# A gated cross-attention and mixture-of-experts layer: where sixteen late tiles of the shared expert are done, and by which counts the last loads wait

## The chip, the cores and the metric

The kernel runs on one core of a Trainium2 chip. The core has five engines that run their own instruction streams and wait for one another by semaphores: TensorE (PE, matmuls), VectorE (DVE), ScalarE (ACT), GpSimd (POOL) and SyncE (SP, which here only reads registers and issues DMAs). The metric is the device time of one execution in microseconds (us), lower is better. Before the change the median of three runs is 305.51 us (304.73 to 306.84).

## The reference

`x` holds 2 x 1024 tokens of 256 numbers. The layer adds gated cross-attention to it, and then a gated feed-forward part: a shared expert for all tokens, and two of eight experts for each token.

```python
x = x + tanh(g_xattn) * attention(layernorm(x), ctx)        # 16 heads, 64 keys
h = layernorm(x)                                            # 2048 tokens
scores = sigmoid(h @ W_gate_router)
sel = top_k(scores + expert_bias, 2); w = scores[sel] / sum(scores[sel])
shared = silu(h @ Wg_s) * (h @ Wu_s) @ Wd_s                 # hidden width 192
routed_k = silu(h @ Wg[sel_k]) * (h @ Wu[sel_k]) @ Wd[sel_k]
x = x + tanh(g_ffn) * (shared + w_0 * routed_0 + w_1 * routed_1)
```

## The kernel before

All arithmetic is in float32; where more speed is wanted, an operand is split into a high and a low part of the faster format and three products are made of them (`split_product`). Tokens are worked on in T = 16 tiles of 128.

**Token loop.** Each of the steps t = 1 to 15 (`token_loop`, one `step(t, q)` for each engine) interleaves several tiles: TensorE transposes tile t+2, makes the shared expert's hidden layer and the router's logits of tile t-2 (`shared_up`), transposes the probabilities of tile t, makes the scores of tile t+2 and the attention output of tile t. In the last two steps there is no tile t+2 any more. Behind the loop tiles 14 and 15 are finished: second layer norm, `shared_up`, the choice of experts, the counting of places (`rank`, `count`), and the tables that say which expert each expert tile has and where its rows lie (`tables` on VectorE). GpSimd writes each token's normalised row to `rows_dram`, once for each of its two experts, at its place in the expert's area.

**Late tiles.** The hidden layer of the shared expert stays in SBUF (`late_hid`) for all tiles. What is left of a tile is late work: TensorE transposes the hidden layer (`late_transpose`, two transposes), ScalarE copies that to `lhT` (`late_hidden`), TensorE multiplies by `Wds` (`late_down`, two matmuls), ScalarE copies the result to `late_out` (`late_copy`), GpSimd adds it to `x_sb` (`late_add`). Tiles 0 to NB - 1 = 11 go this way between the token loop and the expert loop. `late_out` is the same memory as `plane[1]`, below.

**Expert loop.** `expert_loop` runs over SLOT_TILES = 39 places for expert tiles of 128 rows (steps j = -4 to 40; the number that hold rows depends on the data). For each tile SP loads 128 gathered rows, at an address that it reads from `tile_src` four tiles ahead; TensorE transposes them, multiplies by the expert's weights, ScalarE and VectorE make the hidden layer, TensorE multiplies by `Wd` (step j + 2), ScalarE copies the result to one of four buffers, and GpSimd scatters it by an indirect DMA to `routed_dram`, which has a row for each token and choice. Semaphores `scattered[0]` to `scattered[3]` count the scatters of each buffer.

**Planes and tail.** Then SP loads `routed_dram` back in chunks of PLANE = 4 token tiles, first the first choice (plane 0, in order of expert number), then the second (plane 1). Before each load it waits until enough tiles are scattered: `turns[c]` holds four counts, which VectorE worked out in steps 1 to 3 from the places that chunk c's tokens occupy (`tiles_up_to`, `last_turns`, `count_turns`), and which SP reads from SBUF into registers, four reads for a row (`turn_values`). The counts of plane 0 leave out expert 7, which nobody has as first choice. Plane 1 has one row of counts for all four chunks, the largest of all:

```python
sp.wait_ge(scattered[r], turns[min(n, T // PLANE)][r])   # n = 0..3 plane 0, 4..7 plane 1
```

For tiles 0 to 11 VectorE adds both planes to `x_sb` with the tokens' weights (`add_low` for plane 0, L1328 for plane 1), and the pairs of tiles are stored. Tiles 12 to 15 go another way: their late work is done in steps 39 and 40 and behind the loop, their product stays open in PSUM, and TensorE adds three more products to it (`tail_sum`, L1442): the identity times the `x_sb` rows, and two diagonal matrices of the weights (`diag`, made by ScalarE in steps 32 to 39) times the planes. ScalarE copies the sums (L926) and the last stores follow. SP issues two of the eight stores, ScalarE six.

**What sets the order.** Each engine does its instructions in the order in which this code issues them; SP's register reads, waits and DMA issues stand in one such order too. There is no scheduler.

## Time and profile before

| | before |
|---|---|
| median of the runs | 305.51 us |
| lowest and highest run | 304.73 and 306.84 us |
| span of the profiled execution (first to last instruction) | 304.1 us |
| TensorE busy | 274.8 us (90%) |
| VectorE busy | 239.4 us (79%) |
| GpSimd busy | 172.6 us (57%) |
| ScalarE busy | 160.7 us (53%) |
| DMA traffic | 49.74 MB |

The profile shows one execution, with times in us from the start of its span; that execution is not one of the timed runs. A share of busy time is a mean over stages: up to about 160 us the token loop, to 197 us the end of routing and the late tiles, to 292 us the expert loop, and the tail to 304. What a change in one of them is worth is read from the waits in that stage.

### The profile page before, as it was taken

The numbers are of one execution on the slowest core, as the hardware profiler recorded it, in microseconds if no ns is written. First come the engines' busy times: TensorE is split into PE (matmuls) and PEld (weight loads), VectorE is DVE, ScalarE is ACT, GpSimd is POOL, SyncE is SP. The second block draws the span as 40 slices with busy tenths as digits, with TensorE's granted clock in tenths as the row PEclk, the third lists the DMA queues.
The fourth block names the chain that finished last, engine by engine and source line by source line (L and its number), as shares of the span: only waits on it lengthen the run. The fifth ranks groups of instructions, "written<-read, shape, count | busy, mean of one in ns | idle before, by whom it ended". The sixth has DMA issues, their size and how long they took to land.

```text
span 304.1 us, 6562 instructions
## 1 busy us (share of the span) xinstructions
PE 274.8 (90%) x1746; PEld 246.3 (81%) x1747; DVE 239.4 (79%) x691; ACT 160.7 (53%) x414; POOL 172.6 (57%) x234
## 2 busy tenths in 40 slices
PE   2899989999999999999996668988799999999994
PEld 1788767998897898999886657877699899999883
DVE  0489989899899789899989565479877777777684
ACT  1452475656666566564453433654455555566731
POOL 8012225777758886897855876648544344444430
PEclk9999999999999999999999999999999999999999
DMA  6999994123359999923121122323343434446796
GB/s 185 361 288 314 306 293 140 41 77 100 103 167 302 312 286 318 270 69 106 35 70 56 59 81 90 105 56 86 90 118 111 123 96 122 121 114 167 249 325 232
DMA packets 45006, 49.74 MB, mean 164 GB/s; under 512 B 3928, under 2 KB 41650, under 8 KB 44978
## 3 DMA queue, kind: packets, MB, share of 16 engines
q1 hardware_dynamic: 39938, 39.37, 45.5%
q0 software_dynamic: 3408, 8.46, 8.1%
q10 hardware_dynamic: 1632, 1.57, 1.5%
q8 instruction: 13, 0.21, 0.3%
q14 instruction: 15, 0.12, 0.1%
HBM read 21.67 MB, written 28.64 MB: 165 GB/s over the span
## 4 chain that ended last, share of the span: by engine, by line
PE 60%; DVE 24%; issue 8%; ACT 4%; DMA 2%; SPq 1%; ACTq 0%; DVEq 0%
PE bank L1401 7%; PE bank L1403 6%; PE bank L1402 5%; PE scores_ps L1401 5%; PE scores_ps L1403 4%; PE scores_ps L1402 4%; DVE row_max L1146 3%; DVE probs L1152 3%; DVE row_sum L1136 3%; PE bank L1347 3%; DVE pT_lo L1129 3%; PE scores_ps L1438 2%; PE bank L1598 2%; DMA Wq_sb<-in_L_xattn_Wq_dram 2%; PE bank L1438 2%
## 5 line engine op out<-in xcount | busy, mean ns | idle before, releaser
L699 POOL DMA_INDIRECT routed_dram<-probs,sct_idx x39 | 38.1, 977 | 49.3 <-ACT probs L911 46.8
L649 POOL TENSOR_TENSOR probs<-probs,row_inv 128x1024 f32<-128x1024 f32 x16 | 30.5, 1909 | 26.4 <-DVE row_inv L1140 26.3
L613 POOL DMA_INDIRECT rows_dram<-xn,slot_i x32 | 32.0, 1000 | 14.0 <-issue 10.5
L1401 PE MATMUL bank<-AB_hi,pT_hi 128*128 128x256 f32 x128 | 37.0, 289 | 2.4 <-DVE pT_lo L1129 2.4
L1403 PE MATMUL bank<-AB_hi,pT_lo 128*128 128x256 f32 x128 | 35.8, 279 | 0.0
L1402 PE MATMUL bank<-AB_lo,pT_hi 128*128 128x256 f32 x128 | 35.7, 279 | 0.0
L768 ACT ACTIVATE probs<-probs 128x1024 f32<-128x1024 f32 x16 | 17.0, 1061 | 29.5 <-DVE probs L1152 25.4
L1401 PE MATMUL scores_ps<-AB_hi,xnT_hi 128*128 128x512 f32 x64 | 27.0, 421 | 2.5 <-DVE xnT_lo L1122 2.3
L1401 PEld LDWEIGHTS bank<-AB_hi,pT_hi 128*128 128x128 f32 x128 | 24.1, 188 | 3.0 <-issue 2.9
L1403 PE MATMUL scores_ps<-AB_hi,xnT_lo 128*128 128x512 f32 x64 | 25.3, 395 | 0.0
L1402 PE MATMUL scores_ps<-AB_lo,xnT_hi 128*128 128x512 f32 x64 | 25.3, 395 | 0.0
L1129 DVE TENSOR_TENSOR pT_lo<-bank,pT_hi 128x512 fp32r<-128x512 f32 x32 | 20.5, 682 | 5.6 <-ACT pT_hi L776 5.3
L1402 PEld LDWEIGHTS bank<-AB_lo,pT_hi 128*128 128x128 f32 x128 | 24.1, 188 | 0.0
L1403 PEld LDWEIGHTS bank<-AB_hi,pT_lo 128*128 128x128 f32 x128 | 24.1, 188 | 0.0
L1299 DVE TENSOR_TENSOR xnT_lo<-bank,xnT_hi 128x256 fp32r<-128x256 f32 x39 | 16.6, 425 | 6.9 <-ACT xnT_hi L888 5.8
L776 ACT ACTIVATE pT_hi<-bank 128x512 fp32r<-128x512 f32 x32 | 17.3, 595 | 6.6 <-PE bank L1500 6.4
L1152 DVE TENSOR_TENSOR probs<-scores_ps,row_max 128x1024 f32<-128x1024 f32 x16 | 19.5, 1216 | 0.1
L1136 DVE TENSOR_REDUCE row_sum<-probs 128x16 f32<-128x1024 f32 x16 | 19.4, 1210 | 0.1
L1146 DVE TENSOR_REDUCE row_max<-scores_ps 128x16 f32<-128x1024 f32 x16 | 19.2, 1200 | 0.0
L1401 PEld LDWEIGHTS scores_ps<-AB_hi,xnT_hi 128*128 128x128 f32 x64 | 12.0, 188 | 6.7 <-DVE xnT_lo L1122 4.5
L1401 PE MATMUL bank<-W_hi,xnT_hi 128*128 x40 | 15.4, 386 | 1.9 <-DVE xnT_lo L1299 1.9
L1401 PE MATMUL scores_ps<-W_hi,xnT_hi 128*128 x38 | 14.6, 384 | 2.6 <-DVE xnT_lo L1299 2.6
(248 smaller groups left out, 876.6 us busy)
## 6 DMA issues: line engine op xcount, KB each, us to landing
rows_dram<-pad_rows SPq DMA_DIRECT2D x10, 1040.0 KB, 16.5
rows_dram<-pad_rows SPq DMA_DIRECT2D x8, 780.0 KB, 12.2
AB_free<-routed_dram SPq DMA_DIRECT2D x8, 512.0 KB, 6.4
probs<-rows_dram SPq DMA_DIRECT2D x30, 130.0 KB
raw_buf<-in_L_ffn_Wg_dram SPq DMA_DIRECT2D x8, 192.0 KB, 2.5
raw_buf<-in_L_ffn_Wu_dram SPq DMA_DIRECT2D x8, 192.0 KB, 2.6
out_dram<-x_sb ACTq DMA_DIRECT2D x6, 256.0 KB, 2.9
pT_hi<-rows_dram SPq DMA_DIRECT2D x9, 130.0 KB
```

Of the source, the lines that this page charges most:

```text
L613: nc.gpsimd.indirect_dma_start(rows_dram[:, :], bass.IndirectOffsetOnAxis(ap=slot_i[:, t, k:k + 1], axis=0), xn2[:, t % KEEP, :], None).th ...
L649: nc.gpsimd.tensor_tensor(pr, pr, row_inv[:, :].unsqueeze(2).to_broadcast([P, H, KV]), ALU.mult).then_inc(norm_done, 1)
L699: nc.gpsimd.indirect_dma_start(routed_dram[:, :], bass.IndirectOffsetOnAxis(ap=sct_idx[(k - 2) % (2 * RING)][:, 0:1], axis=0), y_sb[ks][:, ...
L768: nc.scalar.activation(prob[m % 2][:, :], prob[m % 2][:, :], ACT.Exp).then_inc(exp_done, 1)
L776: nc.scalar.activation(pT_hi[:, 4 * h:4 * h + 4, :], pT_ps[h][:, :].rearrange("p (c s) -> p c s", c=4), ACT.Copy).then_inc(pT_hi_done, 1)
L1129: nc.vector.tensor_tensor(pT_lo[:, 4 * h:4 * h + 4, :], pT_ps[h][:, :].rearrange("p (c s) -> p c s", c=4), pT_hi[:, 4 * h:4 * h + 4, :].bi ...
L1136: nc.vector.tensor_reduce(row_sum[:, :], prob[m % 2][:, :].rearrange("p (h k) -> p h k", k=KV), AX_X, ALU.add).then_inc(sum_done, 1)
L1146: nc.vector.tensor_reduce(row_max[:, :], by_head, AX_X, ALU.max).then_inc(max_done, 1)
L1152: nc.vector.tensor_tensor(prob[u % 2][:, :].rearrange("p (h k) -> p h k", k=KV), by_head, row_max[:, :].unsqueeze(2).to_broadcast([P, H, KV]),
L1401: nc.tensor.matmul(out_ap, a_hi, b_hi, start=first, stop=False)
L1402: nc.tensor.matmul(out_ap, a_hi, b_lo, start=False, stop=False)
L1403: return nc.tensor.matmul(out_ap, a_lo, b_hi, start=False, stop=last)
```

## The change

All late work is done ahead of the expert loop; none is left behind it. In parts:

- Late tiles 0 to 3 (EARLY) are done inside and right behind the last two token steps, with other PSUM banks, `lhT` for two tiles at once, and copies of two tiles at once into parts of `late_hid` that are no longer needed (`late_row`). Tiles 4 to 15 take the places of tiles 0 to 11 between the loops. GpSimd adds all sixteen in steps 0 to 7.
- NB is 10 instead of 12: TensorE sums six tiles (10 to 15), VectorE adds the planes of ten. A sum now starts with the `x_sb` rows (`tail_rows`) and takes the planes' products (`tail_plane`); rows and plane 0 of tiles 10 to 14 stand in steps 39 and 40. GpSimd makes the twelve diagonals, two per step behind the scatters of steps 32 to 37.
- Plane 1 has a row of counts for each chunk. SP reads the four rows in the tail, each in front of its chunk's load.
- SP reads the first four tile addresses before it waits for the scattered rows. TensorE counts the last batch before the wide sum (`last_ps`) instead of after it.

```diff
-NB = 12
+NB = 10
+EARLY = 4
...
-        CHUNK_ROWS = T // PLANE + 1
+        CHUNK_ROWS = TOPK * T // PLANE
...
             sp.wait_ge(tile_src_done, 1)
-            for r in range(KEEP):
-                sp.wait_ge(rows_put[r], 16 * TOPK * T // KEEP)
             sp.wait_ge(pads_put, 16)
...
                     sp.load(src_regs, tile_src[0:1, bass.ds(n, RING)])
                     sources[:] = [sp.snap(r, min_val=0, max_val=PAD_TILE * P) for r in src_regs]
+                if isinstance(n, int) and n == 0:
+                    for r in range(KEEP):
+                        sp.wait_ge(rows_put[r], 16 * TOPK * T // KEEP)
...
                     n = k * (T // PLANE) + c
-                    if n == T // PLANE - 1:
-                        turns.append(turn_values(chunk_turns[0:1, T // PLANE, :]))
+                    if k:
+                        turns.append(turn_values(chunk_turns[0:1, n, :]))
                     for r in range(RING):
-                        sp.wait_ge(scattered[r], turns[min(n, T // PLANE)][r])
+                        sp.wait_ge(scattered[r], turns[n][r])
                     if k:
-                        sp.wait_ge(late_added, NB)
+                        sp.wait_ge(late_added, T)
                     load_plane(sp, k, c * PLANE, PLANE, (plane1_loaded if k else plane0_loaded)[c])
...
+            def weighted_ident(n):
+
+                nc.gpsimd.tensor_scalar(diag[n], ident[:, :], weight[:, NB + n // 2, n % 2:n % 2 + 1], None, ALU.mult).then_inc(diag_done, 1)
...
-                    for z in range(max(0, 2 * j), min(2 * j + 2, NB)):
+                    for z in range(max(0, 2 * j), min(2 * j + 2, T)):
                         late_add(z)
+                n = 2 * (j - (SLOT_TILES - T + NB - 1)) if isinstance(j, int) else -1
+                if 0 <= n < 2 * (T - NB):
...
+                    weighted_ident(n)
+                    weighted_ident(n + 1)
...
+            def early_hidden(z):
+                act.wait_ge(lhT_ps_done, z + 2)
+                after(act, late_done, z)
+                nc.scalar.activation(lhT_both[:, :, :, :].rearrange("p q k s -> p (q k) s"),
+                                     scores_ps[0:FH, 512:1024].rearrange("p (k s) -> p k s", k=4), ACT.Copy).then_inc(lhT_done, 2)
+
+            def early_copy(z):
+                act.wait_ge(late_done, z + 2)
+                act.wait_ge(lhT_ps_done, ((z + 2) * D + F - 1) // F)
+                nc.scalar.activation(used_hid[:, z * D:(z + 2) * D], scores_ps[:, 0:512], ACT.Copy).then_inc(late_read, 2)
...
+                    if t == T - 2:
+                        early_hidden(0)
                     if t == T - 1:
+                        early_hidden(2)
+                        early_copy(0)
                         round_down(3)
...
-                chain(nc.vector.tensor_reduce(chunk_slots[:, T // PLANE:], chunk_turn.rearrange("o c e -> o (c e)"), AX_X, ALU.max))
+                chain(nc.vector.tensor_reduce(chunk_slots[:, T // PLANE:], chunk_turn, AX_X, ALU.max))
...
-                    late_transpose(NB)
-                    late_transpose(NB + 1)
+                    tail_rows(NB)
+                    tail_rows(NB + 1)
                 if isinstance(j, int) and j == SLOT_TILES + 1:
-                    late_down(NB)
-                    late_transpose(NB + 2)
-                    late_down(NB + 1)
+                    for z in range(NB + 2, T - 1):
+                        tail_rows(z)
+                    for z in range(NB, T - 1):
+                        tail_plane(0, z)
...
             expert_loop(pe, expert_step)
-            late_transpose(NB + 3)
-            late_down(NB + 2)
-            late_down(NB + 3)
+            tail_rows(T - 1)
+            tail_plane(0, T - 1)
             for z in range(NB, T):
-                tail_sum(z, ident[:, :], x_sb[:, z, :])
...
+                tail_plane(1, z)
```

How the order moves is shown at three places. The first is SP's queue behind its last gather for the expert loop. `AB_free<-routed_dram` is a plane load, `chunk_turns` a read of one count (four for a row, each followed by two register instructions). Before:

```order
L408 DMA AB_free<-routed_dram 128x4x256 x3
L487 TENSOR_LOAD chunk_turns
L487 ISA x2
...
L408 DMA AB_free<-routed_dram 128x4x256 x5
L402 DMA out_dram<-x_sb 128x2x256 x2
```

And with the change, where the left-out lines are the other three reads of a row:

```order
L414 DMA AB_free<-routed_dram 128x4x256 x4
L493 TENSOR_LOAD chunk_turns
L493 ISA x2
...
L414 DMA AB_free<-routed_dram 128x4x256
L493 TENSOR_LOAD chunk_turns
L493 ISA x2
...
L414 DMA AB_free<-routed_dram 128x4x256
L408 DMA out_dram<-x_sb 128x2x256
```

The one row of counts stood between the third and the fourth load; now a row stands in front of each of the last four.

The second place is TensorE's queue from step 40 on. L1411 ends an expert tile's last product; `lhT` and `late_hid` with `ident` are late work, `x_sb` with `ident` the rows of a sum, and `late_hid` with `AB_free` a diagonal with a plane. Before, from the late work in front of the last expert tile:

```order
L1438 MATMUL bank<-Wds,lhT 128x256 x2
L1431 MATMUL bank<-ident,late_hid 96x128 x2
L1438 MATMUL scores_ps<-Wds,lhT 128x256 x2
...
L1411 MATMUL bank<-AB_hi,pT_lo 128x256
L1431 MATMUL bank<-ident,late_hid 96x128 x2
L1438 MATMUL scores_ps<-Wds,lhT 128x256 x2
L1438 MATMUL bank<-Wds,lhT 128x256 x2
L1442 MATMUL bank<-x_sb,ident 128x256
L1442 MATMUL scores_ps<-x_sb,ident 128x256 x2
```

With the change, from the same place to the end:

```order
L1467 MATMUL scores_ps<-x_sb,ident 128x256 x2
L1467 MATMUL bank<-x_sb,ident 128x256
L1473 MATMUL bank<-AB_free,late_hid 128x256 x2
L1473 MATMUL scores_ps<-AB_free,late_hid 128x256 x2
L1473 MATMUL bank<-AB_free,late_hid 128x256
...
L1434 MATMUL bank<-AB_hi,pT_lo 128x256
L1467 MATMUL bank<-x_sb,ident 128x256
L1473 MATMUL bank<-AB_free,late_hid 128x256 x3
L1473 MATMUL scores_ps<-AB_free,late_hid 128x256 x2
L1473 MATMUL bank<-AB_free,late_hid 128x256 x2
```

Late work has left the tail; rows and plane 0 of the sums moved ahead of the last expert tile, and behind it stand one tile's rows and plane 0 and then the six products with plane 1.

The third place is TensorE's queue in token step 15. L1500 transposes the probabilities, the `Wsh` rows are `shared_up`, the `mask` and `carry` rows `rank`, `bank<-ident,xn` the transposes of a normalised tile. Before:

```order
L1500 MATMUL bank<-ident,probs 128x128 x8
L1401 MATMUL bank<-AB_hi,pT_hi 128x256
...
L1464 MATMUL bank<-carry,ones_r 128x16
L1401 MATMUL bank<-Wsh_hi,xn2T_hi 128x392
...
L1431 MATMUL bank<-ident,late_hid 96x128 x4
L1471 MATMUL bank<-ident,xn 128x128 x2
```

With the change:

```order
L1531 MATMUL bank<-ident,probs 128x128 x8
L1461 MATMUL scores_ps<-Wds,lhT_both 128x256 x2
L1424 MATMUL bank<-AB_hi,pT_hi 128x256
...
L1495 MATMUL bank<-carry,ones_r 128x16
L1461 MATMUL scores_ps<-Wds,lhT_both 128x256 x2
L1454 MATMUL bank<-ident,late_hid 96x128 x2
L1424 MATMUL bank<-Wsh_hi,xn2T_hi 128x392
...
L1461 MATMUL scores_ps<-Wds,lhT_both 128x256 x2
L1454 MATMUL bank<-ident,late_hid 96x128 x2
L1502 MATMUL bank<-ident,xn 128x128 x2
```

A late product now stands ahead of the attention of tile 15, one with two transposes behind the ranking, and another such pair where two pairs of transposes stood. In step 14 there are, in the same manner, four transposes ahead of the attention, and a product with four transposes behind it.

## Rows read from the trace of the kernel before

**Rows 1.** Chain that ended last, tail: start, us, what it went through.

```profile
292.45 0.22 PE bank L1431 x2
292.66 0.87 PE scores_ps L1438 x4
...
298.28 0.86 PE scores_ps L1442 x4
299.14 0.45 PE bank L1442 x2
299.59 0.66 ACT x_sb L926 x2
```

**Rows 2.** A stretch: us, busy (count) of PE, PEld, DVE, ACT, POOL; granted clock; DMA.

```profile
220.00:280.00 60.00, 59.51 (x410) 56.72 (x410) 44.15 (x163) 35.46 (x113) 26.28 (x27) 1.00 0.41 117
```

**Rows 3.** SP's plane loads: start, us, queue, line (the first of x2 starts there).

```profile
278.00 0.38 SPq L408 DMA_DIRECT2D AB_free<-routed_dram  x1
...
286.11 0.36 SPq L408 DMA_DIRECT2D AB_free<-routed_dram  x1
287.51 0.98 SPq L408 DMA_DIRECT2D AB_free<-routed_dram  x2
289.29 0.38 SPq L408 DMA_DIRECT2D AB_free<-routed_dram  x1
```

**Rows 4.** Reads of turn counts between 279 and 282 us: ns, first and last start.

```profile
L487 SPq TENSOR_LOAD <-chunk_turns x4: 267/278/340, 279.5 to 281.3; - x4
L487 SPq SEQ_ASSERT  x4: 18/18/23, 280.1 to 281.8; - x4
```

**Rows 5.** Issue to landing: the last plane load; then the last four stores.

```profile
DMA to landing us min/median/max: 7.2/7.2/7.2
DMA to landing us min/median/max: 2.2/2.9/3.4
```

**Rows 6.** Timeline around the tail: start, us, instruction, idle before and its releaser.

```profile
282.94 0.97 POOL L699 DMA_INDIRECT routed_dram<-probs,sct_idx  x1 [1.15 <-ACT probs L911]
...
291.50 0.47 PE L1407 MATMUL bank<-AB_hi,pT_lo 128*128 x1
292.12 1.67 DVE L1328 SCALAR_TENSOR_TENSOR x_sb<-AB_free,weight,x_sb 128x256 f32<-128x256 f32 x4 [0.91 <-DMA AB_free<-routed_dram]
...
300.28 0.39 ACTq L402 DMA_DIRECT2D out_dram<-x_sb  x1
```

**Rows 7.** An early stretch by engine, and eight transposes early and late.

```profile
3.00:5.00 2.00, 0.00 (x0) 0.00 (x0) 0.00 (x0) 0.00 (x0) 1.88 (x2) 1.00 0.96 284
6.80 1.97 PE L1357 MATMUL bank<-ident,Wq_sb 128*128 128x128 f32 x8 [0.67 <-DVE bias_cols L938]
170.61 1.04 PE L1500 MATMUL bank<-ident,probs 128*128 128x128 f32 x8
```

**Rows 8.** TensorE in the last token steps: first matmuls after an idle time.

```profile
169.42 0.45 PE L1401 MATMUL bank<-Wsh_hi,xn2T_hi 128*128 128x392 f32 x1 [1.29 <-DVE xn2T_lo L1103]
172.71 0.35 PE L1401 MATMUL bank<-AB_hi,pT_hi 128*128 128x256 f32 x1 [1.07 <-DVE pT_lo L1129]
178.11 0.45 PE L1401 MATMUL bank<-Wsh_hi,xn2T_hi 128*128 128x392 f32 x1 [1.68 <-DVE xn2T_lo L1103]
```

**Rows 9.** The expert loop's start: SP's last wait, first gather, TensorE's first transposes.

```profile
L492 SPq EVENT_SEMAPHORE  x1: 28/28/28, 193.1 to 193.1; - x1
194.50 0.37 SPq L504 DMA_DIRECT2D probs<-rows_dram  x1
197.46 0.60 PE L1598 MATMUL bank<-ident,probs 128*128 128x128 f32 x4
```

**Rows 10.** Additions on GpSimd beside VectorE's index operation, and that operation alone.

```profile
209.73 1.44 POOL L689 TENSOR_TENSOR x_sb<-AB_free,x_sb 128x256 f32<-128x256 f32 x2
210.39 0.80 DVE L1309 SCALAR_TENSOR_TENSOR sct_idx<-probs,tile_e 128x1 int32<-128x1 f32 x1
219.63 0.21 DVE L1309 SCALAR_TENSOR_TENSOR sct_idx<-probs,tile_e 128x1 int32<-128x1 f32 x1
```

More of the change, by code:

```diff
@@ L87, in flamingo_layer @@
         Wds = sb("Wds", [FH, 2, D])
-        lhT = [sb(f"lhT{q}", [FH, 2, P]) for q in range(2)]
+        lhT_both = sb("lhT_both", [FH, 2, 2, P])
+        lhT = [lhT_both[:, q, :, :] for q in range(2)]
         ident = sb("ident", [P, P])
@@ L1320, in _ @@
             expert_loop(dve, expert_step)
-            for c in range(NB // PLANE):
+            for c in range((NB + PLANE - 1) // PLANE):
                 if c:
@@ L1325, in _ @@
                 dve.wait_ge(plane1_loaded[c], 16)
[L1326 removed]
+                for t in range(c * PLANE, min((c + 1) * PLANE, NB)):
                     dve.wait_ge(plane0_added, t + 1)
```

116 lines of the change are left out of this document (61 added, 55 removed).

## The prediction, made before the changed kernel ran

> **What bounds the kernel now.** I read the chain that ended last first, from its end. After the last tile of the expert loop it runs through TensorE alone: late tiles (L1431 two transposes, L1438 the product with `Wds`), then the twelve sums of L1442, then ScalarE's copies [rows 1]. So the end hangs on TensorE. The table by stage says the same of the loop: 59.5 of 60 us busy between 220 and 280 us [rows 2]. From the loop's end the profile gives prices: a late tile costs TensorE 0.87 us for its product and 0.22 for its transposes, a sum 0.43 to 0.45 [rows 1].
>
> Next I read SP's queue, because it issues the eight plane loads (0.5 MB each). Plane 0's chunk 0 goes at 278.0 and its chunk 3 at 286.1; plane 1's chunks 0, 1, 2, 3 go from 287.5 to 289.3, three steps in 1.78 us, so 0.59 from each to the next [rows 3]. The one row of four turn counts that SP reads here (L487) lies between plane 0's chunk 2 and chunk 3, from 279.5 to 281.8: 2.3 us for four reads [rows 4]. It costs nothing there, since chunk 3 goes only at 286.1, when the expert tiles that it needs have been scattered.
>
> Then landings. Plane 1's chunk 3 lands 7.2 us after its issue at 289.3, so at 296.5 [rows 3, 5]. TensorE's last four sums are its last 4 x 0.43 = 1.7 us before 299.6, so from 297.9 [rows 1]: that load has 1.4 us to spare. From the last sum (299.6) to the end of the span (304.1) are 4.5 us: copy, store issue at 300.3, a landing of up to 3.4 us [rows 5, 6].
>
> **The change part by part. The turn counts.** Plane 1's chunks now wait each for its own count, read by SP in front of each of plane 1's four loads. I look first at what finer counts can bring. Worked out from the reference's own inputs: the eight experts hold 1943, 28, 2048, 0, 0, 0, 0 and 77 token pairs, so 34 tiles, and expert 7's single tile is the last. Each chunk of 512 tokens has some of the 77 (17, 19, 28 and 13). A count for plane 1 is the largest over all eight experts, hence 34 for every chunk, the number that all four waited for before. Nothing is released earlier. The trace agrees: the scatter of that tile (the 34th) starts at 282.9 [rows 6], plane 1's chunk 0 goes at 287.5, and the three others follow without a wait [rows 3].
>
> What it costs: the reads move behind the issue of plane 0's chunk 3, where nothing hides them. Each of the four loads now comes 2.3 + 0.59 = 2.9 us after the one before: 289.0, 291.9, 294.8, 297.7. Chunk 0's tiles have long been scattered by 289.0. The last load goes at 297.7 instead of 289.3, +8.4 us. (Other rows of reads are not cheaper by more than a tenth or two; I use 2.3.)
>
> How long it then takes to land is not shown for a load with no other close to it. Bounds: 2.2 us, the quickest 256 KB store [rows 5], and 7.2. Between them: plane 1's chunk 0, with others issued 1.4 us before and 0.6 after it, released VectorE at 292.1, 4.6 us after its issue [rows 3, 6]. I take 3.8, since twice a store's bytes must cost more than 2.2 and fewer neighbours less than 4.6. It lands at 301.5, and token tiles 12 to 15 need it.
>
> **The sums.** TensorE has six tiles to sum instead of four, but the x rows and plane 0 come inside steps 39 and 40: three terms for six tiles are 18 x 0.43 = 7.8 us, against 4 late tiles and 12 sums before (4.4 + 5.2 = 9.6). By 295 all is done that does not need plane 1: before, the last expert tile's product began at 291.5 [rows 6]; eight sums (3.4 us) now stand in front of it in place of 2.0 us of late work, and two more sums follow it. VectorE has 20 additions of 0.42 (1.67 for four [rows 6]) instead of 24, 1.7 us less. Neither is worth anything at the end, since both now wait for plane 1. Left after 301.5 are four sums.
>
> **TensorE's rate in those four.** From 295 to 301.5 it has only the two sums that need plane 1's chunk 2. What does it run at after that? The granted clock reads 1.00 (2.4 GHz) everywhere, even between 3 and 5 us, where TensorE had no instruction. But the spacing of equal rows says otherwise: eight 128x128 transposes take 1.97 us at 6.8 us, shortly after the engine's first work, and 1.04 at 170.6 [rows 7]. That is the 1.2 GHz level after idleness. I take the doubled spacing for the four sums: 4 x 0.86 = 3.4 us, ending at 305.0; with the undoubled one 1.7 us, ending at 303.2. The Trainium skill ("TensorE: Matmul & The Clock Gate", Part 1) has the rule for it: the throttled state is the default, and only activity lifts it. By that rule the doubled case holds and the sum below is the higher one; by the granted clock column alone it is the lower. After the last sum I take 3.7 us instead of 4.5, as the final stores have fewer neighbours (2.5 instead of 3.4, between 2.2 and 3.4 [rows 5]). The span's end from this part: 308.7, so +4.6 (undoubled: 306.9, +2.8).
>
> **Four late tiles in the last two token steps.** They go into TensorE's idle times there, which end at 169.4 (1.29 us), 172.7 (1.07) and 178.1 (1.68) [rows 8]. Into the first go a product and four transposes, 0.87 + 0.44 = 1.3; into the second a product, 0.9; into the third a product and two transposes, 1.1. The fourth product and its pair of transposes replace the two pairs that stood ahead of token tile 15's transposes (1.1 for 0.44). The first gap is full, the others nearly: +0.2, between 0 and 0.6. ScalarE's wider copies stand where it waits for TensorE. If this cover is gone, what is late next is the normalised token tile 15, and through it all routing.
>
> **Ahead of the expert loop.** Twelve late tiles are there before and after, in one pattern, and TensorE goes from them to the first expert tile without idling at 197.5 [rows 9]. SP reads the tile addresses before its wait for the scattered rows, not behind it: wait over at 193.1, first gather at 194.5 [rows 9]. Up to 0.9 of these 1.4 us go. But the gather isn't what TensorE waits for, so 0 (bound -0.9). The count before the wide sum: at most 0.1, likewise hidden: 0.
>
> **In the loop.** GpSimd adds all sixteen tiles by step 7, four more than before, 0.72 each. VectorE's index operation takes 0.80 beside such an addition at 210.4 [rows 10] against some 0.2 elsewhere; two such steps, mostly out of phase: +0.1 (0 to 0.6). The diagonals move from ScalarE to GpSimd, two per step behind its scatter. A 128x128 product by GpSimd is not shown; between nothing and the 0.72 of an addition of twice the width. Two at most 1.44 plus 0.97 for the scatter [rows 6] pass the tile's 2.1 us only at that bound: 0 (to +0.5). ScalarE isn't waited for in those steps: 0.
>
> **Sum.** 4.6 + 0.2 + 0.1 = +4.9 on the span of 304.1, so 309.0. The runs' median of 305.51 lies 1.4 above the span; I carry this along: 310.4 us.
>
> **The rivals.** *Full rate*: the same wait for SP, but the sums at 0.43. For it: the granted clock, never under 1.00, and two sums that interrupt the idleness. Against it: [rows 7]. 310.4 - 1.8 = 308.6.
> *Not slower*: SP's reads cost little, because they are quicker there or the sequencer gets ahead. With loads at their old spacing the last one lands by 296.5 and the last four sums end at 298.2 instead of 299.6: -1.4; with +0.3 in front 304.4. It decides at the read: the end stays at 304.1 if the last load lands at 298.4, so goes at 294.6, a quarter of 8.5 us each, 1.5 us for four reads instead of 2.3. For it: only that a single TENSOR_LOAD shows 0.27 us; against it: starts 0.6 apart [rows 4].
> *An earlier loop*: the first gather does decide, and 0.9 come back: 309.5. Against it: no idle time at 197.5 [rows 9].
> *Late token steps*: the inserted tiles and GpSimd's additions cost their upper bounds of 0.6 and 0.6: +0.9 over my sum, 311.3. For it: gaps that are filled to the brim.
>
> **How the numbers follow.** Chances: my sum 0.38, full rate 0.32, late token steps 0.12, earlier loop 0.10, not slower 0.08. The range: full rate with a quick landing (-0.7) and a short store (-0.5) gives 307.4 at the low end; my sum with a landing of 4.6 (+0.8) and the front's bounds (+0.9) gives 312.1 at the high end. Some 2 in 10 are left out, the case "not slower" among them. A measurement of this kernel can tell about 1% (3.1 us, so 308.6) from no change. Slower by over 1%: my sum, the late steps, 0.07 of the earlier loop and half of full rate make 0.73, of which I keep 0.70. Within 1%: the other half of full rate, the rest of the earlier loop and "not slower" make 0.27, of which I keep 0.25. Faster by over 1%: no mechanism gives it; 0.05 for what I have not seen.
>
> **What would show it.** Four reads between each of plane 1's load issues, 2.9 us apart, the last near 298; VectorE and TensorE idle for them; four last sums 0.86 apart (or 0.43); token steps and the loop's start within 0.6 us of before. It is wrong if plane 1's last load goes before 295, or if the end of the span still follows TensorE's sums without a gap.

## The result, and the profile after

The changed kernel takes 312.58 us (median of 4 runs, 311.52 to 312.95), the kernel before 305.12 beside it (304.58 to 306.84). The ratio is 1.023, with a 95% interval of 1.019 to 1.027: the change makes the kernel slower. Predicted were 310.4 us with a range that ended at 312.1. Side and mechanism were right; the size was 2.2 us too small. Here and below the medians are of all runs, while a ratio and its interval leave out the runs that lay over 1.5% above the fastest run of their kernel.

| | before | after |
|---|---|---|
| median of the runs | 305.12 us | 312.58 us |
| profiled execution: span | 304.1 us | 310.1 us |
| first exponential of the token loop starts | 33.57 us | 34.20 us |
| plane 1's last load is issued | 289.29 us [rows 3] | 298.31 us |
| last store is issued | 300.28 us [rows 6] | 307.48 us |
| granted clock, mean of the span | 1.000 | 0.981 |

From the page of after: the span, TensorE's granted clock in 40 slices, and two of the queues (packets, MB, share).

```profile
span 310.1 us, 6641 instructions
...
PEclk9999999999999999999999999999999999999975
...
q8 instruction: 13, 0.21, 0.3%
```

The row of the clock ends in 7 and 5; in the page of before, which the prediction had read, it stands at 9 to the end. The queue q8 comes back below.

SP's timeline in after (start, us, queue, line): plane 0's last load and plane 1's four. They answer to [rows 3].

```profile
285.86 0.36 SPq L414 DMA_DIRECT2D AB_free<-routed_dram  x1
...
288.67 0.36 SPq L414 DMA_DIRECT2D AB_free<-routed_dram  x1
...
291.43 0.36 SPq L414 DMA_DIRECT2D AB_free<-routed_dram  x1
...
294.17 0.36 SPq L414 DMA_DIRECT2D AB_free<-routed_dram  x1
...
298.31 0.36 SPq L414 DMA_DIRECT2D AB_free<-routed_dram  x1
```

Three steps of 2.7 to 2.8 us, as predicted (2.9), and a last one of 4.1. What fills them are SP's reads of the counts: in after, those of the third row and of the fourth (ns: min, median, max; first and last start).

```profile
L493 SPq TENSOR_LOAD <-chunk_turns x4: 261/266/285, 291.8 to 293.5; - x4
...
L493 SPq TENSOR_LOAD <-chunk_turns x4: 265/634/934, 294.6 to 297.0; - x4
```

The third row's reads answer to [rows 4]: 0.27 us for one read, 0.57 from one to the next. The fourth row has a read of 0.93.

The last load's landing (DMA view of after: KB, median us to landing), against 7.2 in [rows 5]:

```profile
AB_free<-routed_dram SPq DMA_DIRECT2D x1, 512.0 KB, 4.8
```

TensorE's sums with plane 1 in after (timeline: start, us, tile, count of matmul instructions, two for a sum; idle time before them and its releaser), then stretches of 10 us (busy time of PE, PEld, DVE, ACT, POOL; granted clock, DMA share, GB/s):

```profile
299.40 2.05 PE L1473 MATMUL bank<-AB_free,late_hid 128*128 128x256 f32 x4 [5.90 <-DMA AB_free<-routed_dram]
303.28 2.04 PE L1473 MATMUL scores_ps<-AB_free,late_hid 128*128 128x256 f32 x4 [1.82 <-DMA AB_free<-routed_dram]
305.12 1.91 PE L1473 MATMUL bank<-AB_free,late_hid 128*128 128x256 f32 x4
```

```profile
280.00:290.00 10.00, 9.82 (x63) 8.95 (x62) 7.47 (x26) 4.84 (x15) 9.13 (x13) 1.00 0.58 194
290.00:300.00 10.00, 4.10 (x21) 3.36 (x20) 6.50 (x17) 0.38 (x1) 3.06 (x4) 0.92 0.80 263
300.00:310.00 10.00, 5.20 (x12) 3.14 (x10) 0.17 (x1) 2.30 (x6) 0.00 (x0) 0.50 0.46 153
```

Where TensorE was busy to the last sum before [rows 1], it now stands idle for 5.9 us and again for 1.8, both times for a plane load. The sums then stand 0.92 us apart instead of 0.43, at a granted clock of 0.50, which is the 1.2 GHz level.

One fact is needed for comparing executions: the first exponential of the token loop starts between 31.8 and 34.7 us, whichever kernel runs, and this alone spreads the spans by over 2 us. So times inside the kernel are counted from that exponential from here on:

| us behind the first exponential | before | after | after, another run (e11) |
|---|---|---|---|
| first expert tile's copy | 171.2 | 170.1 | 170.2 |
| plane 0's last load issued | 252.5 | 251.7 | 252.5 |
| plane 1's last load issued | 255.7 | 264.1 | 264.2 |
| last sum ends | 266.0 | 272.8 | 272.9 |
| end of the span | 270.5 | 275.9 | 276.0 |

The loop comes 1.1 us sooner, the last load 8.4 later, the end 5.4 later. Under e6 it turns out that the 1.1 us belong to the profiled execution of before, which came late to its loop, and not to the change; counted from the first expert tile's copy, the end comes 6.4 us later (99.3 in before, 105.8 in after and e11). The other 3.0 of the last load's 8.4 come back behind it: before, it landed among other loads, after 7.2 us, and the stores were crowded too.

### The profile page after: what moved, and what is told of

Same layout as the page of the kernel before. It is cut to its first block, busy times and chain, and to the rows that moved or that the text cites. A ratio compares the mean times of both kernels' runs of the same rounds, so it can differ in the third digit from the quotient of the medians.

```text
span 310.1 us, 6641 instructions
## 1 busy us (share of the span) xinstructions
PE 281.3 (91%) x1758; PEld 250.3 (81%) x1759; DVE 237.8 (77%) x687; ACT 159.7 (52%) x408; POOL 183.0 (59%) x250
## 4 chain that ended last, share of the span: by engine, by line
PE 54%; DVE 23%; issue 8%; DMA 6%; ACT 4%; POOL 3%; SPq 1%; POOLq 0%; DVEq 0%; ACTq 0%
PE bank L1424 5%; PE scores_ps L1424 5%; PE bank L1426 5%; PE bank L1425 5%; PE scores_ps L1426 4%; PE scores_ps L1425 4%; DVE row_max L1169 3%; DVE probs L1175 3%; PE bank L1370 3%; DVE row_sum L1159 3%; DVE pT_lo L1152 3%; DMA Wk_sb<-in_L_xattn_Wk_dram 3%; PE bank L1641 2%; PE bank L1392 2%; POOL rows_dram L620 2%
## 5 line engine op out<-in xcount | busy, mean ns | idle before, releaser
L794 ACT ACTIVATE pT_hi<-bank 128x512 fp32r<-128x512 f32 x32 | 17.3, 595 | 6.6 <-PE bank L1531 6.4
L1531 PE MATMUL bank<-ident,probs 128*128 128x128 f32 x128 | 16.6, 273 | 0.0
```

The lines of the kernel that those rows point to most:

```text
L794: nc.scalar.activation(pT_hi[:, 4 * h:4 * h + 4, :], pT_ps[h][:, :].rearrange("p (c s) -> p c s", c=4), ACT.Copy).then_inc(pT_hi_done, 1)
```

## The experiments

Each ran beside the kernel before, whose medians were 304.99 to 305.58 us. "Last copy" is ScalarE's copy of the last expert product; "tail" runs from its start to the end of the span: 11.6 us in before (292.5 to 304.1) and 17.4 in after (292.7 to 310.1).

### The reads alone: e1, e2, e10, e7

**e1**: after with the old single row of counts for plane 1, read ahead of plane 0's last load.

```diff
...
-                    if k:
-                        turns.append(turn_values(chunk_turns[0:1, n, :]))
+                    if n == T // PLANE - 1:
+                        turns.append(turn_values(chunk_turns[0:1, T // PLANE, :]))
                     for r in range(RING):
-                        sp.wait_ge(scattered[r], turns[n][r])
+                        sp.wait_ge(scattered[r], turns[min(n, T // PLANE)][r])
...
```

> The changed kernel with one edit undone: plane 1 has one row of counts again, read by SP ahead of plane 0's last load. All else stays changed. Theory A (SP's four rows of reads behind plane 0's last load delay plane 1's last load, which then idles TensorE): the last plane load goes near 289 instead of 298.3, TensorE's last sums are 0.43 us apart again, the span ends near 302 to 303, 7 to 8 us under the changed kernel's 310.1 and 1 to 2 under before's 304.1. Rival B (the six sums on TensorE, or the diagonals on GpSimd, make the tail long whatever SP does): the span stays above 307.

307.08 us; ratio 1.003 (0.999 to 1.007). Plane 1's loads go 0.54 apart again, the last 2.2 us behind plane 0's last. TensorE's timeline in e1:

```profile
295.64 1.10 PE L1473 MATMUL bank<-AB_free,late_hid 128*128 128x256 f32 x4 [0.72 <-DMA AB_free<-routed_dram]
297.08 1.10 PE L1473 MATMUL scores_ps<-AB_free,late_hid 128*128 128x256 f32 x4 [0.34 <-DMA AB_free<-routed_dram]
```

With the reads out of the way the idle time is 0.7 instead of 5.9 us, the sums stand 0.43 to 0.5 apart, and nearly all of the loss is gone. The other parts of the change together cost at most 0.7%.

**e2**: the reverse, before with nothing but a row of counts for each of plane 1's loads, read in the tail.

```diff
...
-                    if n == T // PLANE - 1:
-                        turns.append(turn_values(chunk_turns[0:1, T // PLANE, :]))
+                    if k:
+                        turns.append(turn_values(chunk_turns[0:1, n, :]))
...
```

> The kernel before with that one edit alone: a row of counts for each chunk of plane 1, read in the tail. Theory A: plane 1's last load goes near 297.5 instead of 289.3, lands some 4.9 us later, and TensorE, which has been idle by then, ends its four sums near 306; span 308 to 310, +4 to +6 on 304.1. Rival B: under +1.5, since before has no diagonals on GpSimd and four sums only.

310.42 us; ratio 1.012 (1.000 to 1.025). The tail is 16.1 us, 4.5 more than in before; loads at 284.09, 286.90, 289.67, 292.42 and 295.82. TensorE in e2:

```profile
300.53 1.22 PE L1442 MATMUL bank<-AB_free,late_hid 128*128 128x256 f32 x2 [4.13 <-DMA AB_free<-routed_dram]
301.54 1.91 PE L1442 MATMUL scores_ps<-AB_free,late_hid 128*128 128x256 f32 x4
```

So this one edit brings the idle time and the halved rate by itself, without any of the moved tiles.

**e10**: after, with each of plane 1's rows read one load earlier, so that three stand behind plane 0's last load.

```diff
-                    if k:
-                        turns.append(turn_values(chunk_turns[0:1, n, :]))
+                    if T // PLANE - 1 <= n < TOPK * T // PLANE - 1:
+                        turns.append(turn_values(chunk_turns[0:1, n + 1, :]))
```

> After, with the four rows of plane 1 each read one load earlier: the first ahead of plane 0's last load, so that three rows are left behind it. Theory A (what stands behind that load costs 2.3 each): the last plane-1 load goes 2.8 us sooner against plane 0's last one, 9.0 to 9.7 instead of 12.4, and the end 2.5 to 3.0 us sooner. On the row that was slow in after, e2 and e3 (the fourth, 3.4 to 4.1 us from load to load in place of 2.8): if it is slow because of what runs beside it at that time (the stores of the first half and the last scatters, some 8 to 11 us behind plane 0's last load), the fourth row, read now at 5.5 to 8.5, takes 2.8 like the others, and the last load goes at 8.9 or sooner; if it is its place in SP's program, it stays at 3.4 or more, and the last load goes at 9.2 or later.

309.51 us, against 311.45 for after beside it (e11). The last load goes 8.8 us behind plane 0's last one, 12.4 in after and 11.7 in e11: one row less is worth 3.6 and 2.9 us there, more than 2.8, since the fourth row is quick now. It ends at 294.1; all of its four reads take 0.26 to 0.28 us. So its place in SP's program isn't what made it slow. In after, e2 and e11 the slow read starts where GpSimd's last scatter and the first stores are on the way. Which of these slows it was not separated.

**e7**: e1 with its single row behind plane 0's last load.

```diff
-                    if n == T // PLANE - 1:
+                    if n == T // PLANE:
                         turns.append(turn_values(chunk_turns[0:1, T // PLANE, :]))
```

> After, with a single row of turn counts for plane 1 (as in before), but read behind the issue of plane 0's last load instead of ahead of it: one row on the path, where after has four and the earlier run with the row ahead has none. Theory A (each row that is read behind plane 0's last load moves plane 1's loads by its 2.3 us): the first plane-1 load comes 2.8 us after plane 0's last, the three others 0.55 apart, so the last 4.5 after it (2.2 with the row ahead, 12.4 in after); TensorE idles over 2 us ahead of its plane-1 sums, and the end comes 1.5 to 2.4 us later than with the row ahead. Rival B (the loss in after comes from waiting four times, not from the reads): the last load goes within 0.5 us of the run with the row ahead.

Loads: 2.83 us behind plane 0's last one, then 0.54, 0.54 and 0.56, the last 4.47 behind: as the reads' price has it. TensorE in e7:

```profile
296.29 1.10 PE L1473 MATMUL bank<-AB_free,late_hid 128*128 128x256 f32 x4 [3.32 <-DMA AB_free<-routed_dram]
297.67 1.80 PE L1473 MATMUL scores_ps<-AB_free,late_hid 128*128 128x256 f32 x4 [0.27 <-DMA AB_free<-routed_dram]
```

The last store is issued 9.5 us behind the last copy, in e1 6.2. The end did not follow: 305.83 us, not slower than e1 (307.08). Two things hide the row there. Eight of e1's ten runs, but only three of e7's, took 2.4 us or more beyond their spans instead of 1.7 to 1.9, which the section on e11 to e13 explains. And in e1 the profiled span ended 5.2 us behind its last store (2.7 in e7), after a last scatter by GpSimd that took 4.02 us instead of 1.0. What the end waits for there is not a load, a sum or a store, but GpSimd's DRAIN, the instruction with which each engine closes (ns; first and last start). It lasts until 305.2; SP's, which comes last in e7 and in before, was done at 303.0:

```profile
L67 POOLq DRAIN  x1: 10122/10122/10122, 295.1 to 295.1; - x1
L67 SPq DRAIN  x1: 13/13/13, 303.0 to 303.0; - x1
```

So the price of a row is shown at the loads and the sums, not in the median.

### The clock: e3, e5

**e3** and **e5** keep TensorE busy in after while it waits: products into a bank that nobody reads, ahead of the plane-1 sums (20 in e3, 12 in e5, and 5 more ahead of tile 12).

```diff
             tail_plane(0, T - 1)
+            pe.wait_ge(ycopy_done, SLOT_TILES)
+            for n in range(12):
+                nc.tensor.matmul(bank[0][:, 0:D], ident[:, :], x_sb[:, T - 1, :], start=True, stop=True)
             for z in range(NB, T):
+                if z == T - PLANE:
+                    for n in range(5):
+                        nc.tensor.matmul(bank[0][:, 0:D], ident[:, :], x_sb[:, T - 1, :], start=True, stop=True)
                 tail_plane(1, z)
```

> The changed kernel with 25 extra products of 256 columns on TensorE into a spare bank while it waits for plane 1's last two loads; their result is not used. Theory A's second half (TensorE is at the lower clock when the last load lands): the last four sums are 0.43 us apart instead of 0.92, the granted clock stays 1.00 to their end, span 1.5 to 2 us under 310.1. Rival C (the sums are slow for another reason, as waiting on memory): spacing stays 0.9, span within 0.5 us of 310.1.

311.8 us, mean clock 1.000. The last four sums take 0.43 each, but the fillers ended at 302.9 and 305.9, later than the loads landed: the rate was gained and lost again.

> After, with 12 filler products (0.43 us each, into a bank that nobody reads) between the last plane-0 sum and the plane-1 sums of tiles 10 and 11, and 5 more ahead of those of tiles 12 to 15; the earlier run with 20 and 5 kept the clock but its fillers ended later than the landings. Theory A (the four sums run at half the clock because TensorE stood idle while SP read the rows): fillers end before the landings at about 299.4 and 303.2, the last four sums take 0.43 each in place of 0.92, and the tail from the last expert copy to the end falls from 17.4 to 15.4 to 16.0 us; the median falls by 1.4 to 2.0 us against after. Rival B (the landing of the last load alone decides, and the sums at half rate are hidden behind stores): tail unchanged, 17.4 within 0.4.

308.48 us; ratio 1.010 (1.005 to 1.016). TensorE in e5:

```profile
295.06 5.34 PE L1681 MATMUL bank<-x_sb,ident 128*128 128x256 f32 x24
300.81 1.10 PE L1473 MATMUL bank<-AB_free,late_hid 128*128 128x256 f32 x4 [0.41 <-DMA AB_free<-routed_dram]
301.75 2.32 PE L1685 MATMUL bank<-x_sb,ident 128*128 128x256 f32 x10
303.91 1.03 PE L1473 MATMUL scores_ps<-AB_free,late_hid 128*128 128x256 f32 x4
```

The tail falls from 17.4 to 14.7 us. From the issue of the last load to the end of the last sum it takes 6.8 instead of 8.7: 1.9 us, the doubled rate of four sums. The rest of the 2.7 comes from loads that went 0.6 to 1.0 sooner against the last copy in this execution. So useless work makes the kernel faster (the median is also 2.6 us below that of e13, which ran on another chip, with longer code too but without fillers in the tail), and the halved rate is worth 1.9 us of its end. The rival by which the landing alone decides is out.

### The parts that were costed at nothing: e6, e9, e4, e8

**e6**: before, with only SP's read of the source addresses moved ahead of its wait for the rows.

```diff
             sp.wait_ge(tile_src_done, 1)
-            for r in range(KEEP):
-                sp.wait_ge(rows_put[r], 16 * TOPK * T // KEEP)
 ...
+                if isinstance(n, int) and n == 0:
+                    for r in range(KEEP):
+                        sp.wait_ge(rows_put[r], 16 * TOPK * T // KEEP)
```

> Before, with one edit of the change alone: SP reads the source addresses of its first gathers ahead of its wait for the rows, in place of behind it. Theory A (this read stood between the last row and the first gather): the first expert transposes come 0.9 us sooner against the first exponential of the token loop (33.6 in place of 34.5 us behind the first tile's, by the trace: 197.1 less 162.9 against 197.5 less 163.9), and the end as much sooner if nothing else holds it: -0.9 us. Rival B (the 0.9 comes from the shared expert's tiles having been moved, or from PE): the loop starts where it did, 0 within 0.2.

ScalarE's timeline: the first exponential and the first expert copy in before, then in e6.

```profile
33.57 1.05 ACT L768 ACTIVATE probs<-probs 128x1024 f32<-128x1024 f32 x1
...
204.80 0.38 ACT L911 ACTIVATE probs<-bank 128x256 f32<-128x256 f32 x1
```

```profile
33.82 1.05 ACT L769 ACTIVATE probs<-probs 128x1024 f32<-128x1024 f32 x1
...
204.06 0.38 ACT L912 ACTIVATE probs<-bank 128x256 f32<-128x256 f32 x1
```

171.23 us before and 170.24 in e6: the loop starts 1.0 us sooner, and the profiled span counted from the exponential is 269.5 instead of 270.5. The number expected came, but by luck: the gather is not its cause. e2, in which SP has the old order, shows it. Its first exponential, its first gathers and its first expert transposes:

```profile
31.85 1.05 ACT L768 ACTIVATE probs<-probs 128x1024 f32<-128x1024 f32 x1
191.50 1.43 SPq L504 DMA_DIRECT2D probs<-rows_dram  x3
195.73 0.60 PE L1598 MATMUL bank<-ident,probs 128*128 128x128 f32 x4
```

Counted from the exponential, e2's first gather goes 1.3 us sooner than before's (159.65; 194.50 in [rows 9] is 160.93), and its transposes start at the same 163.88 (before 163.89). In e6 the gather goes at 158.32 and the transposes start at 163.01; TensorE comes to them from the late work without idle time in all three. In e6 TensorE was 0.7 us ahead of before already when the last ranking began, at 151.93 instead of 152.64, which is 4.8 us ahead of SP's read of the addresses. Some 9 us earlier VectorE had waited for TensorE in before, and in e6 it had not:

```profile
176.64 0.42 DVE L1109 TENSOR_TENSOR x_sb<-bank,x_sb 128x256 f32<-128x256 f32 x1 [0.76 <-PE bank L1403]
```

```profile
176.00 0.43 DVE L1110 TENSOR_TENSOR x_sb<-bank,x_sb 128x256 f32<-128x256 f32 x1
```

e2 has no such wait, but loses as much in a later stretch ahead of its loop, at a granted clock of 0.51:

```profile
180.60:183.90 3.30, 3.30 (x11) 2.94 (x11) 1.18 (x9) 0.78 (x3) 2.53 (x3) 0.51 0.36 122
```

So the loop hangs on TensorE's late work and not on the first gather, as the prediction had it [rows 9], and the 1.0 us was lost in single executions ahead of anything that the edit touches. Why both executions with the old order lost it, at different places, and none of the fourteen with the new one, stays open. The twelve runs agree that there is no gain: 305.64 us, ratio 1.002 (0.999 to 1.006).

**e9**: after with the diagonals on ScalarE, as in before.

```diff
...
-                    weighted_ident(n)
-                    weighted_ident(n + 1)
...
+                    for m in (n, n + 1):
+                        nc.scalar.activation(diag[m], ident[:, :], ACT.Copy, scale=weight[:, NB + m // 2, m % 2:m % 2 + 1]).then_inc(diag_done, 1)
```

> After, with one edit undone: the twelve weighted diagonals are made by ScalarE, as in before, and not by GpSimd. Theory A (two diagonals of 0.6 each and a scatter of 1.03 make GpSimd's turn 2.44 us, longer than the tiles' 2.13, so that the scatters of tiles 28 to 33 slip by about 1.0 us): the scatters of the last tiles stand 2.1 to 2.2 apart, the first of the SP's four plane-0 chunks to be waited for last is issued about 1.0 us sooner against the last expert copy, and the median falls by 0.8 to 1.2. Rival B (the scatters had 1.3 us in hand, and SP's loads wait for the very last scatter, which is bounded by the last expert product): 0 to -0.3.

On GpSimd two diagonals and a scatter make 2.44 us a tile, more than the tile's 2.13. With ScalarE the scatter of tile 33 does start 1.1 us sooner against the copy of tile 36 (tiles counted from 0; 5.30 ahead of it, 4.24 in after). But plane 0's last load goes at 6.80 us ahead of the last copy, in after 6.82, and the tail is 17.3. By the semaphores in the trace this load waits for the scatter of the tile ahead of that one, 32 (expert 7's tile 33 is left out of plane 0's counts): its last count comes 0.02 us ahead of the load in both. With ScalarE that scatter starts 0.4 us sooner against the copy of tile 36 (7.12 ahead of it, 6.68 in after), but it lands 6.1 us behind its start instead of 5.7, both times beside plane 0's first three loads. Late scatters cost nothing here: the prediction's zero holds, though GpSimd came nearer to the bound than its row let expect. The median of 310.11 (spans of 306.8 to 309.9) is 1.3 below e11's on another chip; the profiled executions don't account for that.

**e4** joins the edits of e1 and e9; **e8** adds three fillers ahead of the plane-1 sums:

```diff
             tail_plane(0, T - 1)
+            pe.wait_ge(ycopy_done, SLOT_TILES)
+            for n in range(3):
+                nc.tensor.matmul(bank[0][:, 0:D], ident[:, :], x_sb[:, T - 1, :], start=True, stop=True)
             for z in range(NB, T):
                 tail_plane(1, z)
```

> As e1_one_row, with the twelve diagonals made by ScalarE instead of GpSimd in the same steps. If GpSimd's diagonals (1.44 us a step beside a scatter of 1.03) hold back the last scatters and with them the plane loads: the scatter of the 34th tile comes about 1 us earlier and the span is 0.5 to 1 us under e1_one_row's. If the tail is set by TensorE's or VectorE's own work: the same as e1_one_row within 0.3 us.

304.81 us; ratio 0.998 (0.994 to 1.002). TensorE in e4:

```profile
292.64 1.10 PE L1474 MATMUL bank<-AB_free,late_hid 128*128 128x256 f32 x4 [1.45 <-DMA AB_free<-routed_dram]
294.02 1.93 PE L1474 MATMUL scores_ps<-AB_free,late_hid 128*128 128x256 f32 x4 [0.28 <-DMA AB_free<-routed_dram]
```

> After with one row of turn counts for plane 1 read ahead of the last plane-0 load, the diagonals on ScalarE (304.81 median as run before, last four sums 1.91 for two tiles), and three fillers of 0.43 us between the last plane-0 sum and the first plane-1 sum, where TensorE stood idle for 1.45. Theory A (1.45 us of idleness lets the clock fall, and the sums of the last four tiles then take twice as long): those sums take 0.43 to 0.5 each and the end comes 1.2 to 1.8 us sooner against the last expert copy: tail 8.6 to 9.2 in place of 10.3, median 303.0 to 303.6. Rival B (the clock falls by itself at the end of the loop, or the sums wait for the stores): tail 10.3 within 0.4.

304.67 us; ratio 1.000 (0.997 to 1.004). The idle time of 1.45 us, filled, gives sums at 0.43 to 0.5 again. But the tail falls only from 10.3 to 9.6: ScalarE's copies and stores (1.1 us for two tiles) are next.

### What lies around the span: e11, e12, e13

> The changed kernel itself, once more, beside the runs above on the same chip: how much of the 2 us between 310.4 and 312.6 belongs to this kernel's tail, and how much to the run. Theory A (the tail was mis-sized: the last load lands 4.8 us after its issue, and the fourth row takes 3.4 to 4.3 us): from the last expert copy to the end 17.4 us within 0.5, spans of 307 to 310 whose spread of some 2 us comes from ahead of the first exponential. Rival B (the profiled execution was an odd one): the tail falls to 16.2 or less, as the sum of the prediction had it, and the median to 310.5 or less with a span within 2 of it.

**e11**, after once more on another chip: 311.45 us (310.41 to 312.05), ratio 1.019 (1.014 to 1.023); tail 16.1 us with a last copy 1.4 later, hence the same end from the first exponential (276.0). So the profile after was not an odd one.

The runs show what they take beyond their spans: 2.5 to 2.75 us in all four of after, 1.7 to 1.8 in 93 runs of before. In the profiles with over 2.4 (after, e1, e8), and in no other, queue q8 moves a packet of 16 KB 1.9 us behind the end of the span (at 311.98, 307.31 and 303.45). In e3 and e5, which only add instructions to TensorE, the queue has 14 packets instead of 13: it brings TensorE's code. **e12** (on e8) and **e13** (on after) shift that code by 64 instructions where TensorE waits for its first load.

```diff
             pe.wait_ge(const_step, 5)
+            for n in range(16):
+                nc.tensor.matmul(bank[1][0:8, 0:8], ident[:, 0:8], ident[:, 0:8], start=True, stop=True)
             pe.wait_ge(ld_ctx, 16 * 4)
```

> The changed kernel with the same 64 instructions at TensorE's start. Theory A: all runs lie 1.7 to 1.9 above their spans, where after's lay 2.5 to 2.75 in four runs and 1.7 to 2.65 in six more; spans stay at 308.6 to 310.2 within the start's spread, so that the median is 310.4 to 311.8. Rival B: some runs lie 2.4 or more above their spans, as before the edit.

> The fillers and diagonals on ScalarE of e8, with 16 products of 8 columns (64 instructions) put ahead of TensorE's first transposes, where it waits until 5.65 us for its first load. Theory A (what lies around the span is 2.5 to 2.8 us when a packet of TensorE's instructions is loaded in the last microseconds, and 1.75 otherwise): the instruction queue q8 shows 14 packets, the last one ahead of 298 us, and all runs lie 1.7 to 1.9 above their spans, where e8's lay 1.7 to 2.8; the median falls by 0.5 to 0.9. Rival B (the figure belongs to the chip or the run): both figures appear again.

The whole page's row of q8 in e13, then its row in the stretch 300 to 302 us:

```profile
q8 instruction: 14, 0.23, 0.3%
...
q8 instruction: 1, 0.02, 3.1%
```

All 18 runs of the two lie 1.7 to 1.9 us above their spans; e8's lay 2.4 to 2.8 in nine of twelve. So a late load of code costs 0.7 to 1.0 us outside the span. No unshifted kernel but before ran on the chip of e12 and e13. But e3 and e5, with the code of their fillers, lay 1.7 to 1.9 us above their spans in all eight runs, on the chips on which 15 of 20 runs of e1 and e4 and nine of twelve of e8 lay over 2.4: the chip alone doesn't make it. The medians: 311.1 us for e13 (e11 311.45), and 305.88 for e12, which did not become faster than e8; its spans are longer instead (303.3 to 305.6 against 300.3 to 305.6).

### The sums ahead of the last product: e14

**e14**: e12 with the plane-0 sums of tiles 10 to 14 behind the last expert product.

```diff
                     for z in range(NB + 2, T - 1):
                         tail_rows(z)
-                    for z in range(NB, T - 1):
-                        tail_plane(0, z)
 ...
             tail_rows(T - 1)
-            tail_plane(0, T - 1)
+            for z in range(NB, T):
+                tail_plane(0, z)
```

> e12 with the plane-0 sums of tiles 10 to 14 behind the last expert product instead of ahead of it (the x rows stay ahead). Theory A (the sums' place delays the last expert copy, its scatter then runs into the plane loads): the last copy comes 2.2 to 2.4 us behind the one before it, not 3.7; the last scatter starts 1.2 to 1.5 us sooner and takes 1.0 us; the last sums end where they did, and the span ends within 4 us of the last store; the median falls by 0.5 to 1.5 against e12, to 304.4 to 305.4, or below before. Rival B (the scatter is not what ends the kernel, the long end is of the run): the copy comes sooner, the median stays within 0.4.

304.89 us (e12: 305.88); ratio to before 0.998 (0.994 to 1.001). GpSimd's last scatter (timeline) in e12, then in e14:

```profile
294.83 4.43 POOL L710 DMA_INDIRECT routed_dram<-probs,sct_idx  x1 [2.74 <-ACT probs L933]
```

```profile
292.76 1.04 POOL L710 DMA_INDIRECT routed_dram<-probs,sct_idx  x1 [1.07 <-ACT probs L933]
```

The last copy comes 2.04 us behind the one before it instead of 3.71, the scatter starts ahead of the crowded stretch, and the span ends 3.3 us behind the last store, in e12 5.0. What ends last in e12 is again GpSimd's DRAIN, which stands behind that scatter, at 305.1; SP's is done at 303.0. In e14 it ends at 302.0, ahead of SP's (303.2). First e12, then e14:

```profile
L67 POOLq DRAIN  x1: 10538/10538/10538, 294.6 to 294.6; - x1
```

```profile
L67 POOLq DRAIN  x1: 9488/9488/9488, 292.5 to 292.5; - x1
```

No version is faster than before by more than a measurement can tell.

## Why the prediction was right in its mechanism and too low by 2.2 us

**Right.** The order of the argument: finer counts release nothing, the reads move onto the path, TensorE waits for plane 1's last load, and the sums behind it run at half rate. e2 makes most of the loss with the reads alone (4.8 of 6.4 us, counted from the first copy), e1 takes it away, and e5 takes the half rate away. Of the two readings of the clock the lower rate was the right one: 0.92 us for a sum in after and 0.43 in e5. The Trainium skill ("TensorE: Matmul & The Clock Gate", Part 1), by which the throttled state is the default and activity lifts it, agrees with that. Of the rivals, full rate and "not slower" are out, the late token steps did not come, and the first gather does not decide (e6). The granted clock agrees as well where it matters, with 0.50 in the last 10 us; only in the start did it mislead: it reads 1.00 there, also from 6.80 to 8.80 us, where eight transposes took 1.97 us [rows 7].

**Terms that were mis-sized.** Span of 310.1 against 309.0:

- *The landing of the last load*, taken as 3.8 us "since twice a store's bytes must cost more than 2.2 and fewer neighbours less than 4.6". It is 4.8 (4.6 to 4.9 in e2, e3, e5 and e9), and the first sum starts 5.0 behind the issue: +1.2. The load has neighbours after all, which the prediction had left out of this step: of the stores, that of 296.82 is still under way, and those of 300.20 and 301.90 start beside it. The three loads before the stores (285.86 to 291.43) took 3.3 to 3.5. That the stores are the reason is argued from these times; no run took them away.
- *The reads*, "Other rows of reads are not cheaper by more than a tenth or two; I use 2.3". Right for three rows; the fourth adds 1.4 (0.6 to 1.6 in the other runs that read it there). From plane 0's last load to plane 1's last one it is 12.45 us, the prediction's times make 11.6: +0.9.
- *The four sums* take 3.75 instead of 3.4, +0.35; from the last sum to the end 3.1 instead of 3.7, -0.6.
- *Ahead of the loop*: 0, with -0.9 as a bound and as a rival. Against before's profiled execution it is -1.1, and -1.0 in e6, but not by the gather: e2's came 1.3 us sooner than before's without any effect. The argument (TensorE doesn't idle at 197.5) held; the execution that the prediction added to had come late to its loop. Of this, 0.9 are left at plane 0's last load in after, nothing in e11.
- *The token steps* (+0.2) and *GpSimd's additions* (+0.1): not found. The first copy comes at 170.1 in after and at 170.2 in e6, which has neither. The idle time of 1.68 us that was to take a product and two transposes [rows 8] follows VectorE's late start in before's execution; it is 0.83 in e6.
- The start of this execution was 0.6 later.

Together: 1.2 + 0.9 + 0.35 - 0.6 - 0.9 - 0.3 + 0.6 = +1.25, by rounding 0.15 more than the 1.1 seen.

**The step that carried the other half**: "The runs' median of 305.51 lies 1.4 above the span; I carry this along". Median and span were of different executions. A run of before lies 1.7 to 1.8 above its own span, and after's four runs 2.5 to 2.75; in the one that was profiled, a packet of TensorE's code is loaded behind the end of the span. That makes 1.1 us. e11, where two of six runs lie so far above their spans, has 311.45.

**The range** reached 0.5 us too short: it took in a landing of 4.6, but neither a slower row of reads nor anything around the span.

## What to carry to other kernels

A threshold that an engine reads from memory before it issues a load costs 0.6 us a value; ask first what the finer value can release, and read it behind something that is awaited anyway. Price what follows a long new wait (5.9 us here) at half of TensorE's rate, and price a late load by the transfers that run beside it then, not by those beside it before. Take span and time from the same execution before adding an offset. Before a gain is put down to an edit, see whether the two executions already differ ahead of it.

## What the runs showed of the hardware that was not expected

- After an idle time the fall of the rate came late. In e4, behind 1.45 us, and in e7, behind 3.32, two sums still ran in 1.10 us at a granted clock of 1.00 and the next took 1.8 to 1.9; in after and e10, behind 5.8 to 5.9, the first two already took 2.04, at 0.50. Behind 0.72 us (e1) nothing fell. The rate came back as well. TensorE in e10:

```profile
299.63 2.04 PE L1473 MATMUL bank<-AB_free,late_hid 128*128 128x256 f32 x4 [5.80 <-DMA AB_free<-routed_dram]
301.47 1.87 PE L1473 MATMUL scores_ps<-AB_free,late_hid 128*128 128x256 f32 x4
303.18 1.03 PE L1473 MATMUL bank<-AB_free,late_hid 128*128 128x256 f32 x4
```

- Loading code isn't always hidden: 0.7 to 1.0 us outside the span, where a packet comes behind its end. The Trainium skill ("Runtime: NRT & Kernel Launch", Instruction fetch mechanics) tells of refills in blocks of 16 KiB, mostly hidden; q8's packets have that size (0.21 MB in 13), and the end of the program is a place where one wasn't hidden.
- One of GpSimd's scatters took 4.0 to 4.4 us instead of 1.0 (e1, e12), both times the last one, beside plane 1's loads and the first stores. GpSimd's closing DRAIN ended 5.9 us behind it and with it the kernel, 2.1 to 2.2 us behind SP's.
- A GpSimd product of a 128x128 tile by a column took 0.6 us (median 614 ns of twelve), more than half of its addition of twice the width (0.72).
